# Transposing weights and quantised rows on VectorE instead of TensorE

## The reference

```
xn  = layernorm(x)
gnn = segment_sum((xn @ W)[src] * edge_weight, dst)       # = A @ (xn @ W), A the 2500 x 2500 matrix of edge weights
q, k, v = xn @ Wq.T + bq, xn @ Wk.T + bk, xn @ Wv.T + bv   # 16 heads of 64
phi(t) = exp(t' @ map) * scale, t' = t / norm(t)           # per head; s = sum over the head of phi(q) * phi(k)
x   = x + gnn + s * v / s
# feed-forward with ternary weights and rows quantised to integers of 8 bits
r   = quantise(layernorm(x)); h = silu(r @ tern(w_gate).T) * (r @ tern(w_up).T)
out = x + quantise(h) @ tern(w_down).T
```

## Time and profile before

| | us |
|---|---|
| median of 3 runs (1676.17 to 1680.43) | 1679.87 |
| the profiled execution | 1680.37 |
| its span, first to last instruction | 1678.6 |
| busy TensorE / VectorE / ScalarE / GpSimd | 1653.2 / 1095.4 / 519.1 / 588.5 |
| mean granted TensorE clock | 0.998 of full speed |

### The profile page before, as it was taken

The page is one execution under the profiler, slowest core; times in us unless marked ns, Lnnn a source line. Parts: engine busy times, 40 slices in busy tenths (PEclk is TensorE's granted clock), DMA queues, the critical chain, the costliest instruction groups (busy, mean ns, idle before and its releaser), DMA issues.

```text
span 1678.6 us, 23146 instructions
## 1 busy us (share of the span) xinstructions
PE 1653.2 (98%) x8036; PEld 1344.9 (80%) x8036; DVE 1095.4 (65%) x2548; ACT 519.1 (31%) x618; POOL 588.5 (35%) x392
## 2 busy tenths in 40 slices
PE   6999999999999999999999999999999999999998
PEld 5899999888888888888877777888788887887665
DVE  7866573576676876656666664476485674764886
ACT  4632210222222111114232222233333333332554
POOL 2011565777776777777677700000000000000000
PEclk9999999999999999999999999999999999999999
DMA  9999878655676755657877747345345345452454
GB/s 295 377 402 348 308 234 263 169 138 124 151 195 167 183 141 149 149 138 191 243 209 192 191 147 205 102 135 137 96 146 136 96 136 145 136 145 62 146 172 123
DMA packets 158003, 302.93 MB, mean 180 GB/s; under 512 B 60241, under 2 KB 95105, under 8 KB 157938
## 3 DMA queue, kind: packets, MB, share of 16 engines
q1 hardware_dynamic: 88302, 222.54, 42.2%
q0 software_dynamic: 61824, 52.62, 15.3%
q10 hardware_dynamic: 7812, 26.97, 5.3%
HBM read 202.88 MB, written 99.20 MB: 180 GB/s over the span
## 4 chain that ended last, share of the span: by engine, by line
PE 91%; DMA 5%; DVE 2%; issue 1%; ACT 1%; SPq 0%; DVEq 0%; ACTq 0%
PE PS L367 23%; PE PS L368 23%; PE PS L366 23%; PE PS L1408 4%; PE PS L1410 4%; PE PS L1409 4%; PE PS L1645 4%; DMA Aside<-A_dense 2%; PE PS L1675 2%; PE PS L1472 2%; DMA xnT<-XT 1%; DMA X<-in_x 1%; PE PS L1624 1%; DVE stats L995 1%; PE PS L1388 0%
## 5 line engine op out<-in xcount | busy, mean ns | idle before, releaser
L706 POOL DMA_INDIRECT A_dense<-wtot,cell x336 | 545.4, 1623 | 229.5 <-DMA A_dense<-wtot,cell 133.9
L367 PE MATMUL PS<-SH,AL 125*125 125x512 f32 x784 | 310.0, 395 | 0.0
L366 PE MATMUL PS<-SL,AH 125*125 125x512 f32 x784 | 308.4, 393 | 1.6 <-DVE AL L1222 1.4
L368 PE MATMUL PS<-SH,AH 125*125 125x512 f32 x784 | 309.8, 395 | 0.0
L366 PE MATMUL PS<-WL,xtH 128*125 128x512 f32 x640 | 252.9, 395 | 0.0
L367 PE MATMUL PS<-WH,xtL 128*125 128x512 f32 x640 | 252.0, 394 | 0.0
L368 PE MATMUL PS<-WH,xtH 128*125 128x512 f32 x640 | 251.6, 393 | 0.0
L1220 DVE TENSOR_TENSOR SL<-S,SH 125x1024 fp32r<-125x1024 f32 x98 | 119.9, 1223 | 166.1 <-ACT SH L895 166.1
L895 ACT ACTIVATE SH<-S 125x1024 fp32r (+1 forms) x98 | 103.9, 1061 | 316.4 <-PE PS L368 316.3
L366 PEld LDWEIGHTS PS<-SL,AH 125*125 125x125 f32 x784 | 145.9, 186 | 39.8 <-DVE AL L1222 3.1
L367 PEld LDWEIGHTS PS<-SH,AL 125*125 125x125 f32 x784 | 146.1, 186 | 36.0
(11 more groups left out here) (190 smaller groups left out, 2547.9 us busy)
## 6 DMA issues: line engine op xcount, KB each, us to landing
A_dense<-zeros POOLq DMA_DIRECT2D x40, 1280.0 KB, 8.3
xt<-xnT SPq DMA_DIRECT2D x60, 500.0 KB, 6.1
Araw<-A_dense SPq DMA_DIRECT2D x100, 250.0 KB, 2.7
Aside<-A_dense SPq DMA_DIRECT2D x100, 250.0 KB, 2.9
keyrow<-key_rows SPq DMA_DIRECT2D x42, 512.0 KB, 4.1
ewrow<-weight_rows SPq DMA_DIRECT2D x42, 512.0 KB, 5.6
...
```

What stands on the lines that cost most here:

```text
L366: nc.tensor.matmul(o, lh, rl, start=start, stop=False)
L367: nc.tensor.matmul(o, ll, rh, start=False, stop=False)
L368: return nc.tensor.matmul(o, lh, rh, start=False, stop=stop)
L706: pool.indirect_dma_start(cells[m], bass.IndirectOffsetOnAxis(cell[:, col:col + 1], 0), wtot[:, col:col + 1], None, compute_op=ALU.add).th ...
```

## The change

TensorE loses three kinds of transposes: Wv (64 in float32), the ternary chunks (96) and the integer rows (160). In their place VectorE transposes 32x32 blocks in one instruction (`turn_blocks`), and the DMAs that write the result to memory put the blocks in place by quarters (`store_turned`, four DMAs) or by eighths (`store_halves`, eight). What they leave out of order is put right when read: for Wv by ScalarE and VectorE, which read rows in blocks and write columns of WH and WL; for the ternary weights by TensorE's access pattern; for integer rows by a ScalarE copy (`rows_in_order`).

- Wv is transposed at the end of VectorE's step of tiles 10 to 17 of the map stage. The last two source tiles and the first two of stage 4 are done by halves of columns (`half_products`), and VectorE's order in the first tile of stage 4 changes.
- The ternary chunks move from stage 4 to group 0 of the aggregation (`CHUNKS_AT` chunks per pair of sources), loaded and stored from GpSimd's queue. Their mean is still taken in stage 4. SP loads the result in group 1.
- Integer rows of groups 0 to 3 are transposed by VectorE after the pair of sources in which they were quantised, stored and fetched by ScalarE's queue; those of the last group by SP's.
- Feed-forward: `down` runs one tile later, the hidden transposes after a whole gate and up.
- Four edge pairs move from the map stage to earlier steps, and scatters of empty columns go.

```diff
-EDGE_PLAN = [1] * TILES + [0, 0, 0, 0, 1, 1, 1, 1] + [0, 1, 1, 0, 1, 1, 0, 1] + [1, 0, 1, 0, 1, 0, 1, 1] \
-    + [1, 1, 1, 1, 1, 1, 0, 0] + [4] + [2] * KT + [3] * (TILES - KT) + [4] * 18 + [0] * 2
+EDGE_PLAN = [1] * TILES + [0, 0, 0, 0, 1, 1, 1, 1] + [0, 1, 1, 1, 1, 1, 0, 1] + [1] * KT \
+    + [1, 1, 1, 1, 1, 1, 0, 0] + [4] + [2] * KT + [3, 3] + [3, 2] * (KT // 2) + [3, 3] + [4] * 18 + [0] * 2
...
+CHUNKS_AT = (0, 0, 1, 1, 2, 1, 2, 1, 2, 2)
...
+    def across_blocks(ap):
+        return ap.rearrange("p (k b j) -> p b k j", b=4, j=32), lambda o: o.rearrange("p (b k j) -> p b k j", b=4, j=32)
+
+    def turn_blocks(out_, in_):
+        order_in, order_out = across_blocks(in_)
+        return nc.vector.transpose(order_out(out_), order_in)
+
+    def store_turned(eng, dram, rows, sem):
+        for a in range(4):
+            eng.dma_start(dram.rearrange("(b i) (a f) -> a i b f", b=4, a=4)[a],
+                          rows[a * 32:(a + 1) * 32, :].rearrange("p (b f) -> p b f", b=4)).then_inc(sem, 16)
+
+    def store_halves(eng, dram, rows, sem, down):
+        for a in range(4):
+            for c in range(2):
+                if down:
+                    to = dram.rearrange("(b i) (c a f) -> c a i b f", b=4, c=2, a=4)[c, a]
+                else:
+                    to = dram.rearrange("(b i) (a c f) -> c a i b f", b=4, c=2, a=4)[c, a]
+                eng.dma_start(to, rows[a * 32:(a + 1) * 32, :].rearrange("p (b c f) -> p b c f", b=4, c=2)[:, :, c]).then_inc(sem, 16)
 
     def wait_stage4(eng):
...
+    def integer_rows(i):
+        return rc[:, i, 0:D // 2].bitcast(BF16)
+
+    def turned_rows(i):
+        return rc[:, i, D // 2:D].bitcast(BF16)
+
+    def store_rows(eng, g, d):
+        n = g * GT + d
+        eng.wait_ge(s_turn, n + 1)
+        eng.wait_ge(s_rqst, 64 * n)
+        store_turned(eng, rqT_d[bass.ds(n, 1)].rearrange("o p n -> (o p) n"), turned_rows(d % 2), s_rqst)
+
+    def fetch_rows(eng, g, d):
+        n = g * GT + d
+        eng.wait_ge(s_rqst, 64 * n + 64)
+        eng.wait_ge(s_rqin, 16 * n)
+        eng.dma_start(rqB[:, bass.ds(n, 1), :].rearrange("p o n -> p (o n)"),
+                      rqT_d[bass.ds(n, 1)].rearrange("o p n -> (o p) n")).then_inc(s_rqin, 16)
 
...
+                sp.wait_ge(s_vtr, j + 1)
+                store_turned(sp, wvT_d[j], turned[:, :], s_vout)
...
+        for hh in range(2, HALF + 2):
+            load_next_A(hh)
         for f in range(3):
-            load_next_A(f + 2)
+            for i in range(2):
+                sp.wait_ge(s_fout[i], 128 * (2 * f + 2))
             sp.dma_start(wT[:, f], wT_d[4 * f:4 * f + 4].rearrange("c p n -> p c n")).then_inc(s_wT, 16)
-        with sp.Fori(5, GROUPS * HALF - 1) as hh:
+            load_next_A(HALF + 2 + f)
+        with sp.Fori(HALF + 5, GROUPS * HALF - 1) as hh:
             load_next_A(hh)
...
+        for t in range(TILES - 1):
             write_rows(t, t // 2, t % 2)
+            if t + 2 < TILES - GT:
+                load_r(t + 2, t % 2)
+            if t + 1 in ROUNDED_AT:
+                store_rows(sp, GROUPS - 1, ROUNDED_AT.index(t + 1))
+            if t in ROUNDED_AT:
+                fetch_rows(sp, GROUPS - 1, ROUNDED_AT.index(t))
...
+        wait_stage4(pool)
+        for i in range(2):
+            pool.wait_ge(s_pe5[i], 1)
+        for c in range(2):
+            load_chunk(c)
+        for c in range(12):
+            if c + 2 < 12:
+                pool.wait_ge(s_fq16[c % 2], c // 2 + 1)
+                load_chunk(c + 2)
+            pool.wait_ge(s_fT[c % 2], c // 2 + 1)
+            store_halves(pool, wT_d[c], gTb[:, c % 2, :], s_fout[c % 2], c >= 8)
 
 
...
+        def high_of_block(j):
+            act.wait_ge(s_wv[int(1 < j < 7)], v_in[j])
+            nc.scalar.activation(v_columns(WH, j), v_by_row(j), ACT.Copy).then_inc(s_vh, 1)
...
         high_of_tile(1, HALF - 1 + PASS)
+        act.wait_ge(s_wk, 1)
+        for j in range(KT // 2):
+            high_of_block(j)
         sources_out(HALF - 1, 0)
         high_of_tile(0, HALF + PASS)
-
...
+        for j in range(KT // 2, KT):
+            high_of_block(j)
+        high_of_tile(0, 1 + 2 * HALF)
+        sums_of_weights(0)
+        high_of_tile(1, 1 + 2 * HALF)
+        sums_of_weights(1)
...
-        with act.Fori(1, HALF) as h:
+        chunk = 0
+        for h in range(1, HALF):
             high_of_pair(0, h)
+            for c in range(chunk, chunk + CHUNKS_AT[h]):
+                act.wait_ge(s_fr[c % 2], c // 2 + 1)
+                if c >= 2:
+                    act.wait_ge(s_fT[c % 2], c // 2)
+                nc.scalar.activation(gqb[:, c % 2, :], gwb[:, c % 2, :], ACT.Identity, bias=neg_round[:, :]).then_inc(s_fq16[c % 2], 1)
+            chunk += CHUNKS_AT[h]
         def move_rows(g):
...
                 high_of_pair(g, 2 + d)
+                if d >= 1:
+                    store_rows(act, g - 1, d - 1)
                 integers(g - 1, d)
+                if d >= 2:
+                    fetch_rows(act, g - 1, d - 2)
...
+            high_of_pair(g, 2 + GT)
+            store_rows(act, g - 1, GT - 1)
+            fetch_rows(act, g - 1, GT - 2)
+            high_of_pair(g, 3 + GT)
+            fetch_rows(act, g - 1, GT - 1)
+            with act.Fori(4 + GT, HALF) as h:
                 high_of_pair(g, h)
...
+        def rows_in_order(t):
+            h, i = divmod(t, 2)
+            act.wait_ge(s_rqin, 16 * t + 16)
+            act.wait_ge(s_q[i], h)
+            nc.scalar.activation(rqT[:, i, :, :].rearrange("p k (a j) -> p k a j", j=32),
...
+            if h * 2 + i + 2 < TILES:
+                rows_in_order(h * 2 + i + 2)
...
+            j = t - V_TURN
+            if 0 <= j < KT:
+                dve.wait_ge(s_stage[j % 2], 32 + 16 * (KT // 2) + 16 * (j // 2) + 16)
+                if j:
+                    dve.wait_ge(s_vout, 64 * j)
+                turn_blocks(turned[:, :], stage[:, j % 2, :]).then_inc(s_vtr, 1)
...
+        def low_of_block(j):
+            dve.wait_ge(s_vh, j + 1)
+            nc.vector.tensor_tensor(v_columns(WL, j), v_by_row(j), v_columns(WH, j).bitcast(F32), ALU.subtract).then_inc(s_vl, 1)
...
+                for j in range(KT // 2):
+                    low_of_block(j)
             low_of_tile(1 - i, PASS + t // 2 + i)
...
-        with dve.Fori(0, 2) as h:
-            for i in range(2):
-                low_of_tile(1 - i, h + 2 * HALF + i)
-                stage4_tile(h, i)
+        stage4_tile(0, 0)
+        low_of_tile(0, 1 + 2 * HALF)
+        stage4_tile(0, 1)
+        for i in range(2):
+            low_of_tile(1 - i, 1 + 2 * HALF + i)
+            stage4_tile(1, i)
...
-            dve.wait_ge(s_rq16[i], g * (GT // 2) + d // 2)
+            if not isinstance(g, int) and d < 2:
+                dve.wait_ge(s_rqst, 64 * g * GT)
+            else:
+                dve.wait_ge(s_rqst, 64 * (g * GT + d - 1))
...
+        def turn_rows(g, d):
+            dve.wait_ge(s_rq16[d % 2], g * (GT // 2) + d // 2 + 1)
+            turn_blocks(turned_rows(d % 2), integer_rows(d % 2)).then_inc(s_turn, 1)
...
+        for h in range(1, HALF):
+            low_of_sources(2 * h, 0, h)
+            for c in range(chunk, chunk + CHUNKS_AT[h]):
+                i, f = c % 2, c // 4
+                dve.wait_ge(s_gw[i], c // 2 * 16 + 16)
+                nc.vector.tensor_scalar(gwb[:, i, :], gwb[:, i, :], wq_sc[:, f:f + 1, 1], 1.0,
+                                        ALU.mult, ALU.min).then_inc(s_fm, 1)
+                dve.wait_ge(s_fm, c + 1)
+                nc.vector.tensor_scalar(gwb[:, i, :], gwb[:, i, :], -1.0, ROUND, ALU.max, ALU.add).then_inc(s_fr[i], 1)
+            low_of_sources(2 * h + 1, 1, h)
+            for c in range(chunk, chunk + CHUNKS_AT[h]):
+                i = c % 2
+                dve.wait_ge(s_fq16[i], c // 2 + 1)
+                if c >= 2:
+                    dve.wait_ge(s_fout[i], c // 2 * 128)
+                turn_blocks(gTb[:, i, :], gqb[:, i, :]).then_inc(s_fT[i], 1)
+            chunk += CHUNKS_AT[h]
+        nc.vector.memset(rc[96:P, :, :], 0.0)
...
             for d in range(GT):
                 quantise_r(g - 1, d)
                 low_of_pair(g, 2 + d)
+                turn_rows(g - 1, d)
...
         for t in range(1, TILES - GT - 2):
-            hidden(t // 2, t % 2)
-            add_down(t - 1)
+            hidden(t)
+            if t >= 2:
+                add_down(t - 2)
+            if t - 1 in ROUNDED_AT:
+                turn_rows(GROUPS - 1, ROUNDED_AT.index(t - 1))
...
+        for t in range(TILES - GT - 2, TILES - 1):
+            hidden(t)
+            add_down(t - 2)
+        hidden(TILES - 1)
...
+        def half_products(i, c):
+            cols = slice(c * 512, (c + 1) * 512)
+            for k in range(KT):
+                last = product3(PS[0:ROWS, 2 * i + c, :], xtH[i][:, k, :], xtL[i][:, k, :], WH[:, k, cols], WL[:, k, cols],
+                                k == 0, k == KT - 1)
+            return last
...
```

(93 more changed lines are left out.)

235 lines of the change are left out of this document (87 added, 148 removed).

## The result

The changed kernel takes 1706.6 us (median of 4 runs, 1702.7 to 1711.6) against 1678.0 (4 runs, 1676.0 to 1680.4) before: ratio 1.0172, 95% interval 1.0155 to 1.019. It is slower, and outside the range that was forecast. The profiled execution has a span of 1709.5 us.

The account below looks back on a forecast made before the run. TensorE was taken as the bound, busy 1653.2 of 1678.6 us. Gains of 16.6 and losses of 11.8 us netted -4.8, forecasting 1675 us (likeliest case 1671 to 1679), range 1664 to 1691.

Parts of the forecast that it names:

- Map stage: Eight float32 Wv transpose groups of 0.87 us leave TensorE, with VectorE's new work covered: -7.0 us.
- T: Time of one new VectorE block transpose over 128x1024: taken as 1.15 us, between 0.75 and 2.4.
- rival C: VectorE's block transpose takes two passes, costing groups 1 to 4, feed-forward and group 0 more: 1694 us, chance 0.08.
- Change of weights: Between source tiles and stage 4, products in halves leave TensorE waiting for VectorE: +0.9 us, ends 0 and 3.
- Stage 4: Twelve ternary chunk transposes of 0.46 us leave TensorE, and VectorE and ScalarE lose work: -5.5 us.
- Group 0: Aggregation: GpSimd's chunk loads and stores, 0.85 us an issue, make TensorE wait, +5.6 us; a memset before the boundary, +0.7.
- rival A: GpSimd keeps up in group 0 (issue of 0.76 us or less), no wait: 1669 or 1665 us, chance 0.24.
- Groups 1 to 4: Aggregation: integers behind four DMA issues and waits for row stores delay quantising: +4.6 us over four groups.
- D: Stores of rows or loads of A land late beside 2 MB moves: 1680 to 1683 us, chance 0.18 with Rival E.
- Feed-forward: Row transposes go, period falls from 5.85 to 5.52 us, less 2.85 of waiting; start 1.3 better: -4.1 us.
- Rival B: GpSimd's queue doesn't keep up in group 0, deciding from 0.93 us an issue: 1688 us at 1.05, chance 0.13.
- Rival E: TensorE reads feed-forward weights slower in runs of 32 elements: 10 us at 10%; chance 0.18 with D.

Follow-up runs that it names:

- e1: Changed kernel with ScalarE's weight sums of tile t before the high part of tile t+2 in stage 4's tiles 0 to 5: 1679.2 us, ratio 1.0007.
- f1: e1 with one weight sum per tile in tiles 0 to 11 and the sums' matmul at tile 16: 1678.8 us, ratio 0.9996.
- g1: On e1 with f1's sums, moved memset, copy and statistics, and spread chunks: row stores issued between the two high parts; 1678.7 us, ratio 1.0004.
- g3: e1 with the stores of rows in groups 1 to 4 issued between ScalarE's two high parts: 1688.4 us, ratio 1.0061.
- h2: g1 with the fourth row store of each group left behind both high parts: 1681.5 us, ratio 1.0007.
- g, h and i kernels: Runs on a second chip, on e1 or g1's base, moving row stores, zr load, wT loads, copy in order or chunks: ratios 0.9959 to 1.0061.
- h1: g1 without its sooner stores, and the feed-forward copy in order ahead of the evacuation of the hidden transposes: 1674.0 us, ratio 0.9959.
- e2: Changed kernel with SP's reloads of weight rows moved behind the store of z and the load of x: 1690.3 us, ratio 1.0061.

## Why the prediction was wrong, by its steps

**Map stage: right.** -7.0 forecast and measured. The block transposes (mean ns of one behind the total):

```profile
L418 DVE STREAM_TRANSPOSE rc<-rc 128x1024 bf16<-128x1024 bf16 x20 | 24.9, 1243 | 13.8 <-ACT rc L984 13.7
...
L418 DVE STREAM_TRANSPOSE gTb<-gqb 128x1024 bf16<-128x1024 bf16 x12 | 14.4, 1227 | 0.0
...
L418 DVE STREAM_TRANSPOSE turned<-stage 128x1024 f32<-128x1024 f32 x8 | 9.9, 1234 | 0.0
```

1.23 to 1.24 us with an overlap of 0.08 is the T = 1.15 that I took. Two passes, rival C, are out. The Trainium skill, "Vector Engine (DVE) Microarchitecture Reference" (3.8 The reshape front-end), says one element per cycle and lane; the trace agrees in that bf16 and float32 take the same 1.23 to 1.24 us.

**Change of weights: right.** +0.9 forecast; TensorE waits 1.0 there after the change, 1.3 in e1, 0.8 in f1.

**Stage 4: the step that failed.** "VectorE and ScalarE lose work: -5.5" looked at how much work goes and not at the order of what stays. That the high part moved from one tile ahead to two stood in the diff. The working has no term for it: no wait was added here, an old one came to stand behind a landing. In place of -5.5 the runs show +31.6 in the row of source and stage 4. The order alone makes 32.3 of it (e1 takes them back), as a ring through SP's queue; without it the row is at -0.7. With the order put back, e1 takes 1679.2 and its profiled span is 1676.6, where I had forecast a span of 1678.6 - 4.8 = 1673.8. That the rest of my sum was only 3 us off in total is in part luck: source and stage 4 came out 3.9 us worse than forecast (-0.7 against -4.6), and the aggregation 3.1 better (+7.8 against +10.9).

**Group 0: mis-sized.** The issue of a store was taken as 0.85 us, from the earlier trace rows. In the trace after:

```profile
L432 POOL DMA_DIRECT2D ternary<-gTb x96 | 52.5, 555 | 10.4 <-DVE gTb L418 10.4
...
L1411 DVE MEMSET rc<- 32x2048 f32 x1 | 1.8, 1765 | 0.5 <-issue 0.5
```

0.55 us: rival A's side of the bound, and GpSimd waits between chunks. Of +5.6, 1.1 us of waiting came. The earlier trace rows had five pieces per partition, the new stores one to four; I had said that this points down, and took only 0.05 off. The issue was cheaper with at most 128 pieces than with 640, 0.55 against at least 0.83. The Trainium skill, "DMA: Bandwidth & Descriptors" (Anatomy of one DMA), says that "you can emit a lot of descriptors before the incremental cost shows up"; on GpSimd's queue the issues here differ by 0.28 us or more, though their bytes differ too, so that the pieces are the cause isn't shown. The memset cost more than its +0.7: 2.4 us of waiting and 8 matmuls at 0.43 behind it, 4 in all. (Rival B's bound of 0.93 us an issue doesn't follow from the working, which gives 0.76.)

**Groups 1 to 4: nearly the size, not the mechanism.** +4.6 forecast; the four groups took 452.2 us against 446.9 before, 5.3 more, of which 1.6 is the low clock behind the memset. The waits listed are ten, 2.7 us in all. g1, g3 and h2 show that taking the issues from ahead of the integers gains nothing; by the rows of the g, h and i kernels it is a landing that sets the price here (the nearest rival was D), which is argued, not shown.

**Feed-forward: period and rounding right, start too good.** The period is 5.51 (5.52 forecast), as between the last hidden transposes here:

```profile
1680.39 0.39 PE L1755 MATMUL PS<-ident,hq 125*128 125x125 bf16 x4
...
1685.90 0.39 PE L1755 MATMUL PS<-ident,hq 125*128 125x125 bf16 x4
```

Its cause was right too: with the copy sooner it is 5.41 (h1). Over the 16 tiles behind tile 1 the periods sum to 16 x 5.51 and 2.9 more, where 2.85 was forecast. The start was mis-sized: I gave 1.3 of gain, but from the start of the stage to the hidden transposes of tile 1 it took 14.9 us against 13.4 before. TensorE waits 0.7 for hq and 1.6 for rqT, and 16 matmuls then take 5.36 us in place of 3.67. This low clock isn't in every execution: behind the same two waits e1 and e2 show 3.67, f1 5.35. Rival E, slow reads of 32-element runs, is out: in undisturbed tiles 16 matmuls of gate and up take 3.67 less 0.15 of overlap, within 0.1 us of the 3.46 of before.
